# A decoder layer on one core: the latents' transposes at other places of the body, the even maxima transposed into the latents' bank, and SB with the first softmax step ahead of NM

## The reference, cut to what matters

```python
x = x + attn(layernorm(x), wq, wk, wv, wo)                  # causal self attention, 32 heads of 16
x = x + xattn(layernorm(x), ctx, Wq_d, W_qk, Wkv_d, Wv_u)   # 16 heads, 1500 keys
x = x + ffn(layernorm(x), gate, kernel, bias, lora_A, ...)  # one 512x512 matmul and a LoRA term

def xattn(Q, K, Wq_d, W_qk, Wkv_d, Wv_u):
    C_q = Q @ Wq_d
    C_kv = K @ Wkv_d                                        # the latents: 1500 x 32 of a batch
    scores = einsum((C_q @ W_qk).reshape(b, n, H, 32), C_kv) / sqrt(32)
    attn = softmax(scores)                                  # exp(scores - maximum) / sum
    return einsum(attn, (C_kv @ Wv_u))
```

## Time and profile before

| | |
|---|---|
| median of 3 runs | 640.66 us (640.52 to 640.9) |
| profiled execution | 639.95 us, of which the span is 638.1 us |
| mean granted clock of TensorE in it | 0.975 |
| PE busy | 578.7 us (91%), 4164 matmul records |
| DVE busy | 408.3 us (64%) |
| ACT busy | 323.3 us (51%) |
| POOL busy | 418.2 us (66%) |

### The profile page before, as it was taken

How to read it: one execution, slowest core, us unless ns; L and a number is a source line. 1 busy time by engine, 2 the same in 40 slices (tenths; PEclk the granted TensorE clock), 3 DMA queues, 4 the chain that set the end, 5 groups by cost and what they waited for, 6 DMA issues and landing times.

```text
span 638.1 us, 11581 instructions
## 1 busy us (share of the span) xinstructions
PE 578.7 (91%) x4164; PEld 311.4 (49%) x4164; DVE 408.3 (64%) x701; ACT 323.3 (51%) x680; POOL 418.2 (66%) x409
## 2 busy tenths in 40 slices
PE   7787797999999899999999999999999999986986
PEld 6435343545446445545446444545446445443444
DVE  2627873678746965687746855688746955657432
ACT  1522445447544745457544745557544745564461
POOL 6002177598758878589758878589758888788000
PEclk9997898999999999999999899999999999998899
DMA  8949601651057201841058101751058101200000
GB/s 325 413 103 348 234 18 42 246 197 47 4 189 275 66 12 37 283 185 41 11 188 299 47 1 34 270 198 42 8 166 326 46 2 37 59 10 1 24 3 14
DMA packets 31579, 77.40 MB, mean 121 GB/s; under 512 B 11297, under 2 KB 24961, under 8 KB 29218
## 3 DMA queue, kind: packets, MB, share of 16 engines
q1 hardware_dynamic: 30854, 75.27, 35.0%
q10 hardware_dynamic: 668, 1.40, 0.6%
HBM read 58.92 MB, written 2.88 MB: 97 GB/s over the span
## 4 chain that ended last, share of the span: by engine, by line
PE 56%; DVE 22%; issue 6%; ACT 5%; POOL 4%; SPq 3%; DMA 3%; ACTq 0%; POOLq 0%; DVEq 0%
PE st_ps L733 10%; PE mx_ps L776 9%; PE pv_ps L748 9%; DVE mx_p L1193 7%; PE mi_ps L504 4%; PE mi_ps L516 4%; POOL acc L1264 3%; ACT p_ring L982 2%; DVE p L1112 2%; PE mi_ps L606 2%; DVE p L1157 2%; PE mi_ps L610 2%; PE mi_ps L523 2%; DVE stats L1057 2%; DVE sm L1155 2%
## 5 line engine op out<-in xcount | busy, mean ns | idle before, releaser
L1264 POOL TENSOR_TENSOR acc<-acc,p_ring 125x448 f32<-125x448 f32 x290 | 350.6, 1209 | 49.5 <-ACT p_ring L982 10.3
L1193 DVE TENSOR_REDUCE mx_p<-mx_ps 128x1 f32<-128x500 f32 x336 | 211.0, 671 | 110.6 <-PE mx_ps L776 109.4
L982 ACT ACTIVATE p_ring<-st_ps 125x448 f32<-125x448 f32 x372 | 184.5, 543 | 140.7 <-PE st_ps L733 132.4
L733 PE MATMUL st_ps<-q_st,c_st 98*125 98x448 f32 x372 | 146.4, 433 | 10.1 <-ACT p_ring L982 8.8
L776 PE MATMUL mx_ps<-c_st,q_st 96*128 96x500 f32 x336 | 139.6, 446 | 12.8 <-DVE mx_p L1193 4.7
L733 PEld LDWEIGHTS st_ps<-q_st,c_st 98*125 98x125 f32 x372 | 65.4, 190 | 99.7 <-ACT p_ring L982 77.4
L748 PE MATMUL pv_ps<-p_ring,c_nat 125*32 125x448 f32 x768 | 94.6, 565 | 1.9 <-ACT ox L863 1.0
L776 PEld LDWEIGHTS mx_ps<-c_st,q_st 96*128 96x128 f32 x336 | 62.4, 193 | 44.7 <-DVE mx_p L1193 19.5
L1272 POOL TENSOR_TENSOR rstd<-mv,eps_col 128x1 f32<-128x1 f32 x24 | 5.0, 207 | 119.6 <-DVE mv L1061 119.2
L523 PE MATMUL mi_ps<-ctx_sb,wkv_sb 128*32 128x375 f32 x480 | 45.6, 500 | 3.8 <-DVE p L1112 3.8
L1264 POOL TENSOR_TENSOR acc<-p_ring 125x448 f32<-125x448 f32 x29 | 33.2, 1144 | 19.7 <-ACT p_ring L982 19.7
(11 more groups left out here) (142 smaller groups left out, 673.1 us busy)
## 6 DMA issues: line engine op xcount, KB each, us to landing
ctx_sb<-in_ctx_t SPq DMA_DIRECT2D x16, 3000.0 KB, 11.1
c_st<-ct_hl SPq DMA_DIRECT2D x192, 46.9 KB, 2.3
q_st<-q_hl SPq DMA_DIRECT2D x90, 56.0 KB, 2.0
x_sb<-in_x SPq DMA_DIRECT2D x8, 256.0 KB, 2.8
out_y<-x3n SPq DMA_DIRECT2D x16, 112.0 KB
wq_sb<-in_wq SPq DMA_DIRECT2D x2, 512.0 KB, 6.2
kern_sb<-in_lora_a SPq DMA_DIRECT2D x1, 1024.0 KB, 14.0
wo_sb<-in_wo SPq DMA_DIRECT2D x1, 1024.0 KB, 18.0
```

The source lines that it names most:

```text
L733: mm(st_bank(unit)[0:KC, 0:HALF], c_st[:, b % 4, t * KT + k * KC:t * KT + (k + 1) * KC], q_st[:, b // 2 % 2, b % 2, half * HALF:(half + 1) ...
L982: act.activation(p_ring[:, unit % PR, :], st_bank(unit)[0:KC, 0:HALF], ACT.Exp, scale=float(L) ** -0.5).then_inc(exp_done, 1)
L1193: ve.tensor_reduce(mx_p[:, p:p + 1], mx_ps[unit % MXB][:, 0:KP], AX.X, ALU.max).then_inc(red_done, 1)
L1264: po.tensor_tensor(dst, first, p_ring[:, unit % PR, :].rearrange("p (h s) -> p h s", s=S), ALU.add).then_inc(acc_done, 1)
```

## The change

Three groups of edits:

1. `CT` of the odd batch ("a") moves from group 1, ahead of `T1`, to the head of group 2, ahead of `K`. `CT` of the even batch ("b") moves from group 5 to group 9, between `T2` with its M piece and `CQ`. Since bank 1 is then released later, `P0` waits for `a_lo` and an earlier `mt_sb` in place of `ct_sb`, and `H` waits for `ct_sb`.
2. In groups 3 and 4 `SB` and `SM0` come ahead of the last M piece and `NM`, and `SM1` comes behind `NM`. The M piece goes to the head of group 4, behind that group's scores and sums.
3. `MT` of an even batch is no longer between `Ah` and `A`. It is issued by PE right behind `A` (`turn_maxima`), into columns 384 to 511 of the bank in which the latents lie in columns 0 to 374. ACT and SP do their parts at the same places of their lists as before. Some waits move to other steps: `V` waits for `s1_sb`, `Y` of pair 6 has the wait that `T3` had, and the last even `MT` waits for `f2_sb`.

No instruction is added or taken out.

The diff:

```diff
--- before.py
+++ after.py
@@ -84,22 +84,21 @@
 
 STEPS = [
     [("Ah", "a"), ("M", 2), ("L0", "n"), ("M", 1), ("A", "a")],
-    [("AS", "a"), ("CT", "a"), ("M", 1), ("T1", "n")],
-    [("K", "n"), ("M", 1), ("Qh", "n"), ("M", 3), ("Q1", "n")],
-    [("WA", "n"), ("M", 1), ("SA", "n"), ("M", 2), ("WB", "n"), ("M", 1), ("NM", "m"), ("SB", "n"), ("SM0", "n"),
-     ("SM1", "n")],
-    [("Ah", "b"), ("MT", "m"), ("SE0", "n"), ("A", "b"), ("AS", "b"), ("SE1", "n"), ("V", "n"),
-     ("SN0", "n")],
-    [("CT", "b"), ("SN1", "n")],
+    [("AS", "a"), ("M", 1), ("T1", "n")],
+    [("CT", "a"), ("K", "n"), ("M", 1), ("Qh", "n"), ("M", 3), ("Q1", "n")],
+    [("WA", "n"), ("M", 1), ("SA", "n"), ("M", 2), ("WB", "n"), ("SB", "n"), ("SM0", "n")],
+    [("M", 1), ("Ah", "b"), ("NM", "m"), ("SE0", "n"), ("MT", "m"), ("A", "b"), ("SM1", "n"), ("AS", "b"),
+     ("SE1", "n"), ("V", "n"), ("SN0", "n")],
+    [("SN1", "n")],
     [("P0", "n"), ("M", 1), ("P1", "n"), ("M", 1), ("P2", "n"), ("P3", "n"), ("XC", "f"), ("M", 1)],
     [("O1", "n"), ("M", 3), ("Y", "f")],
     [("DN", "f"), ("Wh", "n"), ("M", 1), ("W1", "n"), ("M", 1), ("DT", "f")],
-    [("YT", "f"), ("M", 1), ("T2", "n"), ("M", 1), ("CQ", "n"), ("M", 1), ("H", "n")],
+    [("YT", "f"), ("M", 1), ("T2", "n"), ("M", 1), ("CT", "b"), ("CQ", "n"), ("M", 1), ("H", "n")],
     [("NM", "o"), ("T3", "f")],
     [("MT", "o"), ("F1", "f"), ("Fh", "f"), ("F2", "f")],
 ]
 
-BANK = {"Ah": (1, 0), "A": (1, 0), "CT": (1, 0), "MT": (0, 1), "T1": 1, "K": 1, "Qh": 0, "Q1": 0,
+BANK = {"Ah": (1, 0), "A": (1, 0), "CT": (1, 0), "MT": 1, "T1": 1, "K": 1, "Qh": 0, "Q1": 0,
         "SA": (0, 1), "SB": (0, 1), "V": 0, "P0": 1, "P1": 0, "P2": 1, "P3": 0, "O1": 0, "Y": 1,
         "DN": 1, "Wh": 0, "W1": 0, "DT": 1, "YT": 1, "T2": 0, "CQ": 0, "H": 1, "T3": 0,
         "F1": 0, "Fh": 1, "F2": 1}
@@ -524,6 +523,13 @@
                                   ctx_sb[:, slot, c, t * KT:(t + 1) * KT], start=(c == 0), stop=(c == CH - 1))
                 return last
 
+            def turn_maxima(b):
+
+                pe.wait_ge(nm_step, 3 * b + 3)
+                pe.transpose(step_bank("MT", b)[0:2 * ROWT, KG * 128:(KG + 1) * 128],
+                             nm_hl[:, :, :].rearrange("p a j -> p (a j)").bitcast(F32), ident[:, :])\
+                    .then_inc(ps["MT"], 1)
+
             def fill(count, bank_=mx_ps[MXB - 1]):
 
                 for _ in range(count):
@@ -560,7 +566,7 @@
                 elif name == "V":
 
                     if n:
-                        pe.wait_ge(mt_sb, 2 * n - 1)
+                        pe.wait_ge(s1_sb, 4 * n + 4)
                     for c in range(CH):
                         last = mm(o[:, 0:128], xnt[:, c, :], wv_sb[:, c, :], start=(c == 0), stop=(c == CH - 1))
                 elif name == "Qh":
@@ -584,7 +590,11 @@
                     r = int(name[1])
                     if r == 0:
 
-                        pe.wait_ge(ct_sb, 2 * n + 1)
+                        if n:
+                            pe.wait_ge(a_lo, 2 * n + 1)
+                            pe.wait_ge(mt_sb, 2 * n - 1)
+                        else:
+                            pe.wait_ge(ct_sb, 1)
                     if r % 2 == 0:
                         pe.wait_ge(soft_n, 6 * n + 3 * (r // 2) + 3)
                     if r == 1:
@@ -621,6 +631,8 @@
                                       rows_of(xnt[:, k, :], n), start=(c == 0), stop=(c == CH // 2 - 1))
                 elif name == "H":
                     pe.wait_ge(cq_sb, n + 1)
+                    if n:
+                        pe.wait_ge(ct_sb, 2 * n + 1)
 
                     if n >= 2:
                         pe.wait_ge(ln[2], 5 * n - 9)
@@ -639,29 +651,34 @@
                     latents(o, slot, (0, 1))
                     return
                 elif name == "A":
-                    last = latents(o, slot, (2, 3))
+                    latents(o, slot, (2, 3)).then_inc(ps[name], 1)
+                    if n % 2 == 0 and n:
+                        turn_maxima(n - 2)
+                    return
                 elif name == "CT":
                     pe.wait_ge(a_f, n + 1)
                     if n:
                         pe.wait_ge(a_lo, n + 1)
+                    if n % 2 == 0 and n >= 4:
+                        pe.wait_ge(ln[2], 5 * (n // 2) - 9)
                     for k in range(KG):
                         last = pe.transpose(o[0:KC, k * 128:(k + 1) * 128], ct_f[:, k * KC:(k + 1) * KC], ident[:, :])
                 elif name == "MT":
 
-
                     if n % 2 == 0 and n + 2 < B:
-                        pe.wait_ge(s1_sb, 2 * n + 7)
+                        return
                     if n == B - 2:
-                        pe.wait_ge(ct_sb, B)
+                        pe.wait_ge(f2_sb, n // 2 - 1)
                     if n % 2 and n + 1 < B:
                         pe.wait_ge(qh_lo, n // 2 + 2)
-                    pe.wait_ge(nm_step, 3 * n + 3)
-                    last = pe.transpose(o[0:2 * ROWT, 0:128],
-                                        nm_hl[:, :, :].rearrange("p a j -> p (a j)").bitcast(F32), ident[:, :])
+                    turn_maxima(n)
+                    return
                 elif name == "Y":
 
                     if n + 2 >= PAIRS:
                         pe.wait_ge(f2_sb, n)
+                    if n + 2 == PAIRS:
+                        pe.wait_ge(mt_sb, B - 1)
                     pe.wait_ge(ox_sb, 4 * n + 4)
                     for h in range(H):
                         t, q = h % 4, h // 4
@@ -693,8 +710,6 @@
                     last = four_transposes(o, y_t[:, :, :].rearrange("p q s -> p (q s)"))
                 elif name == "T3":
 
-                    if n + 2 == PAIRS:
-                        pe.wait_ge(mt_sb, B - 1)
                     pe.wait_ge(ln[2], 5 * n + 5)
                     last = four_transposes(o, x3n)
                 elif name == "F1":
@@ -947,7 +962,7 @@
 
                     if n:
                         act.wait_ge(m_in[(n - 1) % 2], 32 * ((n - 1) // 2 + 1))
-                    copy(m_t[:, :], o[0:2 * ROWT, 0:128]).then_inc(mt_sb, 1)
+                    copy(m_t[:, :], o[0:2 * ROWT, KG * 128:(KG + 1) * 128]).then_inc(mt_sb, 1)
                     if n == 1:
 
                         act.wait_ge(mt_sb, n + 1)
```

## The result

The changed kernel takes 646.02 us (median of 20 runs, 638.76 to 650.1) against 639.44 us (20 runs, 637.08 to 645.58) of the kernel before. The ratio is 1.0081, 95% interval [1.0062, 1.0099]: slower, where 4.2 us faster was forecast. The medians lie 6.6 us apart; the ratio stands for 5.2 us, since it leaves out runs more than 1.5% above the fastest of their kernel (three of the 20 here, and four of the 12 of the version with the middle alone further down), which are those with the lowest clocks. The profiled execution took 645.27 us, its span is 643.5 us, its mean granted clock 0.952 (before: 0.975).

A forecast was written before the change was run, and what follows sets the result against it. PE was taken as more than half of the chain that ended last, DVE second. The terms -2.3 (bodies 1 to 6), -1.9 (body 0) and 0 gave -4.2 us, from 640.66 to 636.4 us; range 632.8 to 638.7 us.

The forecast's parts named there:

- CT of the even batch: Groups 5 and 6 to group 9: transposes fall into PE's 0.46 us idle ahead of CQ; 0 us.
- five rivals: Groups 4 to 6 gain 0.12; start gives less 0.14; steady gain lost 0.08; nothing adds up 0.05; m row slower 0.04.
- rival B: Body 0: something other than DVE takes over, only T1's 0.8 of 1.9 us remain, 637.5 us; chance 0.14.
- CT(a), steady bodies: Group 1, bodies 1 to 6: PE's idle time ahead of the odd batch's CT, waiting for DVE's AS, goes; -2.3 us.
- Body 0: First body: K 0.8 us earlier, AS 1.7 to 2.1 us earlier, DVE's chain moves with it; -1.9 us in all.
- Groups 4 to 6: Steady bodies: DVE's list to SM1's end keeps the same instructions, so PE's waits only move; 0 us, -1.2 to +0.3 a body.
- MT behind A: Even batches: SP starts the m row 1 us later, with 2 us of room before the scores; 0 us.
- rival E: Bodies 1 to 6: the later m row arrives 1.4 us too late for the scores, 645 us; chance 0.04.
- Body 7: Last body: NM and MT of batch 14 about 1.1 us later, covered by POOL's additions; 0 us, otherwise 1.1 us.

The follow-up runs named there:

- the middle: Kernel before with only SB and SM0 ahead of NM and the even MT behind A, both CT at their old places: 642.16 us, ratio 1.0007.
- the version with three fillers: Changed kernel plus three matmuls whose result nobody reads, at the even batch's old CT place in group 5: 637.94 us, again 638.78 us.
- the kernel before with three fillers: Kernel before plus three matmuls whose result nobody reads, at the head of group 5's steps ahead of CT: 638.46 us, ratio 0.9971.

## Why the prediction was wrong

**The step that failed** is the one on CT of the even batch: "It leaves groups 5 and 6, where PE was waiting for ACT anyway ... and PE nothing. ... 0 us." The wait came out as argued: PE stood 0.69 us ahead of group 6's scores and stands 1.01 us there when CT(b) alone is moved, and the scores still follow the pair ahead of them by 1.92 us. What was wrong is the price of idle time. The sum took the clock as given, at the 0.975 of the profile before. Moving this alone costs 6.7 us, moving it back in the changed kernel wins 5.4, and three idle matmuls in its old place win 8 (of which the kernel before, given the same three, gains 2 as well). None of the five rivals has the clock as something that the edits change; B has a part of body 0 at the lower clock, and the profile before shows it there, but not for the steady bodies.

The mechanism, as far as it is shown: longer waits in groups 4 to 6, lower clock behind them (27.2 instead of 3.4 us in bodies 1 to 6), and with fillers in the second wait less of the lower clock (10.2 us) and no loss. Which executions fall and which don't, with the same waits, is not shown. The Trainium skill says in "TensorE: Matmul & The Clock Gate", Part 1, that the throttled clock is the default and that activity releases it. The trace agrees as far as it goes: the five stretches shown above lie behind waits.

**At equal clock the sum may have been about right.** The lines give 637.9 against 641.9 us, 4.0 us faster; -4.2 was forecast. The first of these lies outside the changed kernel's runs, but the version with three fillers, whose runs do reach 0.97, gives 637.8 and 638.5. The steady bodies say the same: 2.6 us less over five of them outside the low stretches, where 2.3 over six was forecast. Against it stands the kernel before with three fillers, 639.7 at equal clock, to which 1.2 to 1.9 us are left, and at the medians hardly any. The parts are another matter: CT(a) alone gives 1.0 us where 3.1 were forecast, the middle 2.2 where 1.1 was. That the total comes near is in part luck.

**CT(a), steady bodies** (-2.3): right in its rows. No instruction of CT waits for DVE any more, and T1 in body 3 follows an M piece with no idle time, its scores and M pieces behind it too. Made alone it gave nothing in the steady bodies, since PE then waits for SB's copy; the prediction priced it as a gain of its own, and it is one only together with the middle.

**Body 0** (-1.9): too large. T1 first brings K 0.86 us earlier, as forecast (0.8), and the lower clock takes all of it back on K itself. AS begins at 72.65 + 1.15 = 73.80 instead of 74.69, 0.9 us earlier and not 1.7 to 2.1, and PE's M piece ahead of P2 0.46 us earlier; by K of body 1 it is 0.37 us later. It is rival B's case: A ran at the lower clock, as B has it, and AS waited 0.30 us for ACT's copy of `ct_hl`.

**Groups 4 to 6** (0 a body, from -1.2 to +0.3): DVE's list became 0.75 us longer over six bodies, 0.13 us a body and inside the bounds. But the reason was incomplete: SM0's subtraction met POOL's additions and became up to 0.95 us longer, and it stands ahead of NM, so PE waits 0.58 us for MT in body 3. "GPSIMD Engine Reference", section "Specifications", of the Trainium skill says that GpSimd shares its ways into SBUF with VectorE and that DVE's instructions with two inputs there collide with it. The runs agree: 1.09 us with POOL's additions at a quarter, up to 2.04 beside the full ones.

**MT behind A** (0; rival E): right. No scores of bodies 1 to 6 wait for `m_t`. In body 0 they wait 2.18 us, SP having begun at 71.92: 74.67 - 71.92 = 2.75 us, the 2.7 of the earlier trace rows. Against the kernel before they start at 74.67 + 1.15 = 75.82, 0.12 us later than 75.70. Whether a load under way would have held the row up is not tested, since it was through when SP began. The stretches of the changed kernel:

```profile
71.00:72.00 1.00, 1.00 (x15) 0.69 (x8) 0.97 (x2) 0.38 (x2) 0.00 (x0) 1.00 0.89 384
72.00:73.00 1.00, 0.48 (x5) 0.29 (x3) 0.70 (x2) 1.00 (x3) 0.00 (x0) 1.00 0.17 72
```

**Body 7** (0): the MT of batch 14 waits 2.09 us for DVE. This was to be covered by POOL, and POOL has no part in the chain that ended last in the changed kernel (0%). Instead, PE's wait was followed by a low stretch. The part from body 6 to the end is 0.5 us shorter than before all the same, so this term holds none of the loss.

**The precision.** The prediction took 1.3 us as what can be told from no change, by three runs of 640.52 to 640.9 us. Twenty runs of the same kernel go from 637.08 to 645.58 us.

## What to carry to other kernels

Idle time of the engine that bounds a kernel is not free to enlarge. Before work is taken out of a stretch where PE waits, look at the granted clock behind that stretch in several executions, and if it falls there, leave the work in or put idle matmuls in its place. Try the same idle matmuls in the kernel before as well, or their gain is taken for the change's. And when two versions run at different clocks, compare the times run by run against the clock before judging the edit.

## What the runs showed of the hardware

- Two waits of 0.79 to 1.08 and of 1.02 us with 0.9 us of work between them, in a kernel whose PE is 91% busy, are followed by the lower clock in five of the six steady bodies of the profiled execution; with waits of 0.78 to 1.08 and 0.35 us (three executions with fillers) that happened in one or two of six, and with 0.32 and 1.02 us (one execution) in none.
- The same program differs by its clock from run to run: 638.76 us at 0.965, 650.1 us at 0.947. Over all kernels 0.01 of mean clock goes with 2.1 to 5.1 us.
- DVE's subtraction of 128x896 with both inputs in SBUF takes 1.09 us, and from 1.09 to 2.04 us beside POOL's additions. The cast of 128x7 took 0.46 us in body 3 of the kernel before and 0.19 us in the changed one.
